# Two gather stages of a graph layer: one TensorE signal for each pair of tiles, and the sums last in their step

## What is computed

```python
# layer 0
agg = segment_sum(x[src], dst, num_segments=6250)
h1 = (agg + x) @ W1 + b1
# layer 1
s0, s1 = x[src][:, :64], x[src][:, 64:].reshape(-1, 64, 3)
out0 = alpha * (einsum('ei,io->eo', s0 * a0, w_00_0) + inv_sqrt3 * einsum('eim,em,io->eo', s1, a1, w_11_0))
out1 = alpha * (einsum('ei,io,em->eom', s0, w_01_1, a1) + einsum('eim,io->eom', s1 * a0, w_10_1))
agg = segment_sum(concat(out0, out1) * msg_rad, dst, num_segments=6250) / 4
```

## Time and profile before

| | |
|---|---|
| median of 3 runs | 3297.3 us (3295.75 to 3297.57) |
| the profiled execution's own time | 3321.8 us |
| its span in the profile | 3320.2 us |
| mean granted clock of TensorE | 0.918 of full speed |
| first gather, POOL's fetches | 59 to 1072 us |
| second gather, POOL's fetches | 1705 to 2920 us |
| what lies between and behind | dense layers and expert layers |

### The profile page before, as it was taken

One profiled execution on the slowest core, in us unless ns is written; L12 is line 12 of the kernel. 1 busy time (PEld: TensorE's weight loads), 2 busy tenths in 40 slices (PEclk: granted clock), 3 DMA queues, 4 the chain that ended last, 5 costly groups with the idle time before them and its releaser, 6 DMA issues. The chain is left out here.

```text
span 3320.2 us, 52314 instructions
## 1 busy us (share of the span) xinstructions
PE 2798.5 (84%) x14715; PEld 2306.8 (69%) x14715; DVE 1720.7 (52%) x5294; ACT 1425.6 (43%) x3977; POOL 1775.9 (53%) x1889
## 2 busy tenths in 40 slices
PE   1888898899888899799957888888887777779998
PEld 1667777777777788588845555555676666668887
DVE  5742223577665566545544545555555555653333
ACT  4012222244222455255556766676645654532221
POOL 5666666666666155456666666666666566610000
PEclk9999998999998999799978988988888888889999
DMA  7244344666665376345553433433345544442222
GB/s 218 78 118 122 115 125 124 200 200 204 204 204 182 120 237 212 110 142 164 167 156 100 116 108 104 116 107 111 105 136 147 148 138 129 136 124 75 74 74 63
DMA packets 270570, 457.96 MB, mean 138 GB/s; under 512 B 75154, under 2 KB 194685, under 8 KB 269206
## 3 DMA queue, kind: packets, MB, share of 16 engines
q1 hardware_dynamic: 190642, 238.08, 24.1%
q0 software_dynamic: 78912, 215.69, 22.5%
q10 hardware_dynamic: 750, 1.08, 0.1%
HBM read 342.87 MB, written 111.83 MB: 137 GB/s over the span
## 5 line engine op out<-in xcount | busy, mean ns | idle before, releaser
L2616 POOL DMA_INDIRECT g_got<-xm_d,idx x782 | 768.4, 983 | 458.6 <-issue 212.4
L916 POOL DMA_INDIRECT g_got<-xn_d,idx x654 | 655.6, 1002 | 374.7 <-issue 186.9
L2228 PEld LDWEIGHTS ps<-g_hotw,g_got 128*128 128x128 f32 x3128 | 441.6, 209 | 207.7 <-issue 206.5
L2228 PE MATMUL ps<-g_hotw,g_got 128*128 128x128 f32 (+11 forms) x3128 | 469.1, 298 | 132.3 <-issue 67.1
L1300 PEld LDWEIGHTS ps<-g_hot,g_got 128*128 128x128 f32 x2616 | 351.3, 205 | 82.2 <-issue 74.1
L1300 PE MATMUL ps<-g_hot,g_got 128*128 128x120 f32 (+4 forms) x2616 | 362.5, 288 | 46.4 <-issue 35.2
L2671 ACT ACTIVATE g_hotw<-g_hot,g_wr 128x16 f32<-128x16 f32 (+8 forms) x1308 | 299.3, 312 | 49.2 <-DVE g_hot L627 30.8
L2761 DVE TENSOR_TENSOR g_ring<-g_ring,ps 128x84 f32 (+10 forms) x391 | 133.0, 340 | 346.5 <-DMA jobs_d<-gin_hid 158.9
L1481 POOL TENSOR_TENSOR p_ln_rs<-p_ln_pre,neg_half 125x2 f32<-125x2 f32 x50 | 35.1, 703 | 454.5 <-DVE p_ln_pre L1476 454.5
L2901 PE MATMUL ps<-g_half 128*125 128x512 f32 x400 | 228.0, 721 | 44.9 <-ACT g_half L2645 17.1
L1107 DVE TENSOR_TENSOR g_ring<-g_ring,ps 128x40 f32 (+8 forms) x327 | 68.7, 210 | 329.6 <-remote 200.4
(11 more groups left out here) (391 smaller groups left out, 5135.9 us busy)
## 6 DMA issues: line engine op xcount, KB each, us to landing
h_d<-gin_hid SPq DMA_DIRECT2D x23, 1000.0 KB
gin_hid<-h_d SPq DMA_DIRECT2D x23, 1000.0 KB
job_in<-jobs_d SPq DMA_DIRECT2D x54, 258.0 KB
g_got<-xm_d,idx POOLq DMA_INDIRECT x782
p_z<-z_d SPq DMA_DIRECT2D x49, 224.0 KB
g_got<-xn_d,idx POOLq DMA_INDIRECT x654
q_d<-g_qo SPq DMA_DIRECT2D x25, 250.0 KB
g_wqkv<-q_d SPq DMA_DIRECT2D x25, 250.0 KB
```

What stands on the lines that cost most here:

```text
L916: landed.start(e.indirect_dma_start(got[:, k % (2 * GB), :], None, xn_d[0:N, :], bass.IndirectOffsetOnAxis(ap=idx[:, HT + k:HT + k + 1], a ...
L2228: mm = e.matmul(to, rows[j][:, c * P:(c + 1) * P], hotw[:, j, c * w:4 * w].unsqueeze(1).broadcast_to([P, r, n]), start=(j == 0), stop=(j = ...
L2616: landed.start(e.indirect_dma_start(got[:, 2 * (g % GB) + j, :], None, xm_d[0:N, :], bass.IndirectOffsetOnAxis(ap=idx[:, 2 * g + j:2 * g + ...
```

## The change

- `sums` goes from the first place to the last in PE's list of plans, in both stages: within a step all other matmuls now come before the sums.
- The signals of the other PE functions go away, but for those in steps behind the last sums of the stage. A reader of such a product now waits for the `summed` signal of the first sums whose step is not earlier than the product's. In the second stage that is the sums of the same step; in the first it is the same step for a product in an odd step and the next step for one in an even step.
- In the second stage the two signals of `project` (keys, values) become one condition: ACT's `square` waits for both halves before its first read.
- No matmul, transfer, buffer or lag changes.

```diff
+class Shown:
+    def __init__(self, sem, when, lag, summed, sums_at):
+        self.sem, self.summed, self.sums_at = sem, summed, sums_at
+        self.steps = [s + lag for s in when]
+
+    def alone(self, i):
+        return self.steps[i] > self.sums_at[-1]
+
+    def done(self, ins, i):
+        if self.alone(i):
+            ins.then_inc(self.sem, 1)
+
+    def wait(self, eng, i):
+        if i >= 0 and self.alone(i):
+            eng.wait_ge(self.sem, sum(self.alone(k) for k in range(i + 1)))
+        elif i >= 0:
+            self.summed.wait(eng, sum(at < self.steps[i] for at in self.sums_at), "sums")
...
+            SUMS = [s + LEAD for s in GROUPS]
+            def shown(name, when, lag):
+                return Shown(ph.sem(name), when, lag, summed, SUMS)
+            heavy, xturn, kvs = shown("heavy", QKV, 7), shown("xturn", QKV, 8), shown("kvs", QKV, 25)
+            proj = {"kv0": shown("kv0", QKV, 14), "kv1": shown("kv1", QKV, 15), "q": shown("q", QKV, 16)}
+            hturn, up = shown("hturn", UPS, 0), [shown(f"up{q}", UPQ[q], 0) for q in range(4)]
+            rturn, eturn, hidden = shown("rturn", WTS, 2), shown("eturn", EDGE, 1), shown("hidden", EDGE, 5)
...
                     timeline(LAST_STEP,
-                             (GROUPS, [(sums, LEAD)]),
                              (COUNT, [(count, 1)]),
...
-                             ([EDGE[-1]], [(turn_radial, 12)]))
+                             ([EDGE[-1]], [(turn_radial, 12)]), (GROUPS, [(sums, LEAD)]))
...
+            eturn, hidden, rturn = shown("eturn", RAD, 1), shown("hidden", RAD, 5), shown("rturn", CHUNKS, 11)
+            kturn, proj, dots = shown("kturn", KV, 2), shown("proj", KV, 5), shown("dots", KV, 14)
+            rows, turn = shown("rows", P9, 4), shown("turn", F3, 3)
...
                     def square(i):
                         sizes.wait(e, i - 1, "sum")
-                        dots.wait(e, i - 2, "dots")
+                        dots.wait(e, i - 2)
+                        proj.wait(e, i)
                         for q, bank, to, name, copy in ((0, KB, k1, "k", "raw"), (H1, V, v1, "v", "copy")):
-                            proj.wait(e, i, name)
...
-                    timeline(LAST_STEP, (GROUPS, [(sums, LEAD)]), (RAD, [(hidden_of, 5), (turn_emb, 1)]), (CHUNKS, [(turn_radial, 11)]),
+                    timeline(LAST_STEP, (RAD, [(hidden_of, 5), (turn_emb, 1)]), (CHUNKS, [(turn_radial, 11)]),
                              (KV, [(products, 14), (project, 5), (turn_k, 2)]), (MIX, [(mix_wo, 1), (mix_wq, 3)]), (F3, [(turned, 3)]),
-                             (P9, [(product, 4)]))
+                             (P9, [(product, 4)]), (GROUPS, [(sums, LEAD)]))
```

More of the change, by code:

```diff
@@ L840, in load_xn @@
                         xrs.wait(e, i - 2, "t1")
-                        heavy.wait(e, i - 2, "sums")
+                        heavy.wait(e, i - 2)
                         xn_in.start_rows(e, xn[:, i % 2, :, :], spread(xn_d[0:N, :])[:, 2 * i:2 * i + 2, :], i % 2)
@@ L1023, in blank_rows @@
                     def blank_rows(i):
-                        heavy.wait(e, NB - 1, "sums")
+                        heavy.wait(e, NB - 1)
                         e.memset(attr4[96:RR, :, :], 0.0).then_inc(s_z, 1)
@@ L1078, in join_heavy @@
                     def join_heavy(i):
-                        heavy.wait(e, i, "sums")
+                        heavy.wait(e, i)
                         joined.wait(e, i - 1, "add")
@@ L1140, in acc_kv @@
                     def acc_kv(i):
-                        kvs.wait(e, i, "kv")
+                        kvs.wait(e, i)
                         accd.wait(e, i - 1, "acc")
@@ L1284, in sum_heavy @@
                                               counts_of(2 * i + t), start=(t == 0), stop=(t == 1))
-                        heavy.done(mm, "sums")
+                        heavy.done(mm, i)
                     def sums(g):
@@ L2486, in second_gather @@
             kn = ph.steps("kn", "k")
-            dots = ph.steps("dots", "dots")
             s_b = ph.sem("b")
             x_in = ph.landing("xi", XI, 2)
-            rows = ph.steps("rows", "rows")
             biased = ph.steps("biased", "xb")
@@ L2630, in zero @@
                     def zero(b):
-                        rows.wait(e, b - RB, "rows")
+                        rows.wait(e, b - RB)
                         to = ring[:, :, cols(b)]
@@ L2826, in x3_of @@
                         r = i % XR
-                        rows.wait(e, i, "rows")
+                        rows.wait(e, i)
                         biased.wait(e, i, "xb")
@@ L2876, in turn_radial @@
                         ecopy.wait(e, NV * n + NV - 1, "embT")
-                        rturn.done(e.transpose(ps[:, 2, 0:P], rad[:, :], ident[:, :]), "T")
+                        rturn.done(e.transpose(ps[:, 2, 0:P], rad[:, :], ident[:, :]), n)
                     def hidden_of(i):
@@ L2897, in project @@
                         kcopy.wait(e, i, "T")
-                        for bank, name, at in ((KB, "k", 0), (V, "v", INNER)):
-                            squares.wait(e, i - 1, "raw" if name == "k" else "copy")
+                        for bank, copy, at in ((KB, "raw", 0), (V, "copy", INNER)):
+                            squares.wait(e, i - 1, copy)
                             for c in range(DC):
@@ L2942, in product @@
                             mm = e.matmul(to[:, FILLED[k]], ring[:, k, cols(i)], wm[:, k, FILLED[k]], start=False, stop=(k == SL - 1))
-                        rows.done(mm, "rows")
+                        rows.done(mm, i)
                     def turned(i):
```

108 lines of the change are left out of this document (48 added, 60 removed).

## The result

The kernel before took 3297.57 us (median of 11 runs, 3293.13 to 3303.23), the changed one 3310.37 us (11 runs, 3304.16 to 3316.64). The ratio is 1.0037, 95% interval 1.0028 to 1.0047: 12.8 us more, where 19 more were forecast (3316 us).

A forecast was written before the change was run, and what follows sets the result against it. PE, with what it waits for, was taken to bound both gathers. Lost shadow 36.5 us, less 15.4 for the sums' waits and 2 for the first gather, gave 19 us on 3297.3: 3316 us, range 3236 to 3365.

The forecast's parts named there:

- PE's `project` waits for more than 32.1 us: Sign in the second gather's profile: PE's waits at `project` for DVE's and ACT's reads would exceed the 32.1 us before.
- Readers still trail their products by microseconds: Sign: the forecast is wrong if readers' starts no longer trail PE's products by several microseconds.
- The cost of a signal: PE's 798 signals in both gathers: each taken to cost PE 0, with at most 8 us to win.
- Lost shadow: Second gather: sums no longer run during PE's waits at `project`, `turned` and edge network, 0.87 us each: 36.5 us lost.
- what queues behind: Queues behind later readers: `accumulate` gets sums later, its bank is asked for equally later; the shifts cancel, priced at nothing.
- The credit for the sums' waits: Second gather: the sums' waits of 30.8 us get filled with the step's other work; half, 15.4 us, won.
- The first gather: First gather: 3 us lost at products' waits, 5 us won at the sums' waits; net 2 us won.
- The second 0.87 us of each handoff: Second gather: the later `summed` signal might add 0.87 us again per wait, making 73 us; not counted in the forecast.
- One kind of signal mends the late signals: Rival, both gathers: late signals cost; one kind mends half of 117 us of PE's waits, 3239 us, or all, 3180; chance 0.20.
- Refilled sums, hidden handoffs: Rival, both gathers: sums' waits refilled, 41 us, against half the handoff loss, 18 us: 23 us won, 3274 us; chance 0.13.
- Nothing: Rival: readers held by something neither order nor signal count touches; within 0.2%, 3291 to 3304 us; chance 0.20.

The follow-up runs named there:

- run 5: The changed kernel itself, unedited, on another chip of the slower kind, against the kernel before: 3336.25 us, ratio 1.0053.
- run 6: The changed kernel with 748 removed signals made again and read by nobody, slower chip: 3336.69 us, ratio 1.0052 to the kernel before.
- run 10: Kernel before with sums last in both gathers, products signalling for themselves, and DVE's add one step later in the second gather; slower chip: 3325.49 us, ratio 1.0010.
- run 8: Kernel before with sums still first, products without signals, readers waiting for the first sums of a later step; slower chip: 3328.49 us, ratio 1.0030.
- run 7: Kernel before with sums last in their step in both gathers, every product signalling for itself; slower chip: 3331.16 us, ratio 1.0043.
- run 12: Kernel before with sums last in the first gather only, every product signalling for itself; slower chip: 3320.12 us, ratio 0.9995.
- run 2: Kernel before with sums still first, products without signals, readers waiting for the first sums of a later step; faster chip: 2920.55 us, ratio 1.0011.
- run 1: Kernel before with sums last in their step in both gathers, every product signalling for itself; faster chip: 2917.42 us, ratio 1.0000.
- run 9: The kernel before, unchanged, timed and traced again on a slower chip: 3321.07 us, ratio 1.0003.

## Why the prediction was right, and where its steps were off

**The sign and the size were right, the sum was 6 us high.** Forecast 19 us more; measured 12.8 us on that chip and 17.5 us on that of run 5. PE's `project` waits for more than 32.1 us (61.4), `turned` for more than 18.7 (22.8), the sums for less than 28.4 (3.0), as the prediction said. Readers still trail their products by microseconds (5.97 us in the lines above).

**The cost of a signal: right.** Taken at nothing, measured at 0.44 us for 748 (run 6), inside the scatter. The Trainium skill's rule (TensorE: Matmul & The Clock Gate, "The cost: per-tile semaphore tail") that increments are written one after the other would, by an estimate from its 26 ns, have made this 19 us, were PE to wait for each; no run here shows PE waiting for them.

**Lost shadow: there, but paid back.** 36.5 us were forecast. Only `project`'s share of it, 20.0 us, can be compared cleanly. With the add out of the way (run 10) `project` waits 45.9 us against 21.0 before, 24.9 more, and it is the order that does it, as the prediction said. But the sums' waits fall by as much there, 30.9 to 5.2 us, so that all named waits are 51.8 us against 51.9: the forecast loss, lost shadow less half a credit, is not what made the kernel slower. Of the other two, `turned` went from 18.7 to 22.8 us, 4.1 where 10.4 were forecast; the edge network from 15.5 us over both windows to 25.6 + 5.5 + 18.7 + 5.4 = 55.2 us, where 6.1 more were forecast. Its growth in the first window goes with the shared signal and not with the lost shadow: from 1750 to 2400 us it waits for ACT 35.0, 46.7 and 13.7 us in runs 5, 6 and 8, which share (18.4 and 28.1 in runs 5 and 6 without their one long wait), and nowhere in run 7, which doesn't.

**The step that failed** is the one on what queues behind: "`accumulate` itself gets its sums up to the step's other work later, and the bank that it frees is asked for later by the same amount, so that pair of shifts cancels." The bank's part held; the sums wait for `accumulate` 3 us (L2247 for L2780). But DVE runs in order, and the copy behind `accumulate` serves `project`, which was not moved later. The same paragraph names the copy as something that holds `accumulate` up; with the order changed it works the other way round, for DVE then never stands before the copy (run 7). Price: 67.2 - 45.9 = 21 us of waits from 1750 to 2400 us, and 0.0033 of the run, 11 us (runs 7 and 10).

**The credit for the sums' waits was too small, and covered that.** Half of 30.8 us was taken. From 1750 to 2400 us they fell from 30.9 to 5.3 us with order only, and from 28.4 to 3.0 with the change: five sixths and nine tenths. The two errors have opposite signs: from 1750 to 2400 us about 11 us too little credit, and 21 us of waits, 11 us of time, that were put at nothing. This is why the sum came near with a term missing, and that it came so near is luck.

**The first gather: not contradicted.** 2 us won forecast, 0.9995 measured for the order there (run 12), 1.7 us won, and an interval from 4.6 won to 1.3 lost. The shared signal was not tried there alone.

**The second 0.87 us of each handoff, taken at 0 with 36.5 as its bound.** The shared signal alone costs 10 us where signals are late (run 8) and 3 us where they are prompt (run 2), so it is not free; on top of the order it adds 0.0010, unresolved. A likely reason for its small size stands in the trace of run 7, where both products and sums signal: of 373 signals of products from 1750 to 2900 us, 151 come within 0.2 us ahead of a signal of the sums, though the sums' matmuls take 0.87 us. On the prompt chip it is 0 of 404. Where a late signal arrives with the sums' signal anyhow, waiting for the latter costs little; that this is the reason was not tested.

**The rivals.** *One kind of signal mends the late signals* is out, by the change and by run 6. *Refilled sums, hidden handoffs* was half true: refilled they were, and the handoffs paid for it. *Nothing* is excluded on the slower chips, but it is nearly true where signals are prompt.

**What is not settled.** Why PE's signals are late in the gather stages of three chips and prompt on a fourth was not found. It is neither how many there are (run 6) nor on how many semaphores: in the change only the sums signal there, and more than half are late too (151 of 352 are prompt). The slower chips' traces also hold fewer changes of semaphores by DMAs, 15,828 in the kernel before and 16,091 in run 7 against 39,593 in run 1, for the same 270,570 packets; whether these were merged or not recorded was not found, and late signals may belong with it. That late signals are why the order costs is supported by 1.0000 on the prompt chip and 1.0043 on a late one. A rival is not excluded: on the prompt chip the fetches bound the stage (1004 us against a floor of 985), so a loss of PE's would be hidden there for whatever reason. Signals were not made late or prompt on one and the same chip.

## What to carry to other kernels

When a producer moves to the end of its step, look up where its reader stands on its own engine and what stands behind that reader. The bank that comes back at the right time does not help the next instruction in that queue. If you move the producer, move the reader with it: either alone cost 0.16 and 0.43% here, both together 0.10%. And price a handoff by when the reader starts in the trace, not by when the matmul ends; 748 semaphore increments that nobody waited for were worth nothing that could be measured. And don't add up waits for a time: on the first chip 35 us more of them went with a stage as long as before.

## What the runs showed of the hardware

- The same program took 2918 us on one chip and 3297, 3319 and 3321 us on three others: 13 to 14%, far above what any edit here moved. The time is lost in the stages with indirect fetches: 1004 against 1224 us in the second gather, 844 against 1000 us in the first (runs 1 and 9), while the rest, from the first gather's end to the second's start and from the second's end on, takes 614 + 382 and 620 + 380 us.
- On the slower chips two thirds of TensorE's semaphore increments in the gather stages come late, most by no more than 11 us, and often together: 151 of 373 of the products within 0.2 us ahead of one of the sums (run 7). In dense stages of the same run all are prompt, 14 ns after the matmul. On the fast chip all 574, 143 and 753 counted are prompt.
- The granted clock was 0.966 on the fast chip and 0.917 to 0.926 on the slower ones, with PE idle more there: 0.89 where it had 102 of 650 us without work, 0.97 on the fast chip where it had 61 of 650. Idle time alone does not tell it: the changed kernel on the first chip had 117 of 650 us without work at 0.91.
